# A spectral block on one core: the row transform of x from two fp16 parts in 64-row tiles, and a moved channel mean

## The reference

```python
def conv(x):                                    # x: normalised
    bias = x @ bias_w.T + bias_b
    xf = jnp.fft.rfftn(x.reshape(B, H, W, 4, 96), axes=(1, 2), norm='ortho')
    xr, xi = xf.real, xf.imag
    r1 = relu(block_mul(xr, w1[0]) - block_mul(xi, w1[1]) + b1[0])
    i1 = relu(block_mul(xr, w1[1]) + block_mul(xi, w1[0]) + b1[1])
    r2 = block_mul(r1, w2[0]) - block_mul(i1, w2[1]) + b2[0]
    i2 = block_mul(r2, w2[1]) + block_mul(i1, w2[0]) + b2[1]
    return irfftn(complex(r2, i2), s=(H, W)).reshape(B, H, W, C) + bias
out = x + conv(group_norm(x))                   # 32 groups, eps 1e-5
```

## Time and profile before

| | us |
|---|---|
| median of three runs | 431.16 (430.12 to 432.9) |
| the profiled execution | 432.9 |
| its span, first to last instruction | 431.1 |
| PE busy | 401.2 (93%) |
| DVE busy | 283.1 (66%) |
| ACT busy | 228.9 (53%) |
| POOL busy | 84.1 (19%) |

### The profile page before, as it was taken

One profiled execution on the slowest core, in us unless ns is written; L12 is line 12 of the kernel. 1 busy time (PEld: TensorE's weight loads), 2 busy tenths in 40 slices (PEclk: granted clock), 3 DMA queues, 4 the chain that ended last, 5 costly groups with the idle time before them and its releaser, 6 DMA issues.

```text
span 431.1 us, 19365 instructions
## 1 busy us (share of the span) xinstructions
PE 401.2 (93%) x8610; PEld 354.2 (82%) x8610; DVE 283.1 (66%) x696; ACT 228.9 (53%) x514; POOL 84.1 (19%) x72
## 2 busy tenths in 40 slices
PE   4468799999999999999999999999999999998996
PEld 4467689788898889887898889888898889986894
DVE  4697676864677656874668656865568646767425
ACT  2884865257742666356652576437662666426410
POOL 0000002700063000900036000810027000690000
PEclk9759999999999999999999999999999999999999
DMA  7670000270004300180003600161001700040004
GB/s 220 196 240 2 2 3 5 84 249 2 5 28 171 139 3 3 40 292 4 3 5 122 213 2 5 41 238 57 5 3 68 267 3 5 27 161 2 5 3 148
DMA packets 12406, 33.03 MB, mean 77 GB/s; under 512 B 4962, under 2 KB 6532, under 8 KB 12324
## 3 DMA queue, kind: packets, MB, share of 16 engines
q1 hardware_dynamic: 12324, 31.80, 21.0%
HBM read 16.07 MB, written 12.58 MB: 66 GB/s over the span
## 4 chain that ended last, share of the span: by engine, by line
PE 90%; ACT 4%; issue 2%; DVE 2%; DMA 1%; DVEq 0%; SPq 0%; ACTq 0%
PE bank L571 90%; DMA x_sb<-in_x 1%; ACT y L912 1%; ACT junk L900 1%; ACT yraw L892 1%; ACT r L922 1%; ACT biasw L926 1%; DVE o_sb L1114 0%; ACT w2s L926 0%; DVE r L1098 0%; ACT z L932 0%; ACT junk L903 0%; DVE rho L1029 0%; ACT rho L951 0%; DVE z L1029 0%
## 5 line engine op out<-in xcount | busy, mean ns | idle before, releaser
L571 PE MATMUL bank<-biasw,y 128*64 128x384 f16 x1152 | 111.1, 336 | 0.4 <-issue 0.4
L571 PEld LDWEIGHTS bank<-biasw,y 128*64 128x64 f16 x1152 | 93.4, 196 | 2.5 <-issue 1.0
L571 PE MATMUL bank<-w2s,rho 128*64 128x96 f16 x3072 | 84.9, 207 | 0.0
L571 PEld LDWEIGHTS bank<-w2s,rho 128*64 128x64 f16 x3072 | 80.0, 109 | 4.0 <-issue 2.5
L877 POOL TENSOR_TENSOR x_sb<-x_sb,added 128x384 f32<-128x384 f32 x56 | 74.8, 1370 | 0.0
L571 PE MATMUL bank<-w1R,y 128*128 128x192 f16 (+3 forms) x768 | 60.3, 228 | 5.9 <-ACT y L912 3.2
L1029 DVE SCALAR_TENSOR_TENSOR rho<-bank,rho 128x256 f16<-128x256 f32 (+2 forms) x128 | 39.9, 363 | 34.1 <-ACT rho L951 23.1
L932 ACT ACTIVATE z<-bank 128x384 f16<-128x384 f32 x72 | 35.3, 490 | 49.9 <-PE bank L571 48.9
L875 POOL TENSOR_TENSOR x_sb<-x_sb,added 128x384 f32<-128x384 f32 x8 | 8.1, 1009 | 270.5 <-DVE yraw L1085 270.5
L917 ACT ACTIVATE g<-bank 128x384 f16<-128x384 f32 x64 | 30.0, 480 | 53.4 <-PE bank L571 53.4
L571 PE MATMUL bank<-tab,x_sb 128*128 128x128 f32 x384 | 50.6, 287 | 7.7 <-DMA x_sb<-in_x 6.2
(11 more groups left out here) (109 smaller groups left out, 414.8 us busy)
## 6 DMA issues: line engine op xcount, KB each, us to landing
x_sb<-in_x SPq DMA_DIRECT2D x16, 768.0 KB, 6.7
out<-o_sb SPq DMA_DIRECT2D x14, 768.0 KB, 3.7
y<-y SPq DMA_DIRECT2D x24, 128.0 KB, 2.7
out<-o_sb SPq DMA_DIRECT2D x8, 192.0 KB, 1.9
tab<-in_tab SPq DMA_DIRECT2D x1, 672.0 KB, 5.6
o_sb<-in_bias_wt SPq DMA_DIRECT2D x4, 144.0 KB, 2.9
b1raw<-in_b1h SPq DMA_DIRECT2D x1, 384.0 KB, 5.9
tab<-in_tab SPq DMA_DIRECT2D x1, 292.5 KB, 3.0
```

What stands on the lines that cost most here:

```text
L571: return nc.tensor.matmul(o, lhsT, rhs, start=start, stop=stop, **kw)
```

## The change

Five things are changed together.

1. For images 2 to 7 the row transform `p1` is replaced by `p1_rows`: x is split beforehand into two fp16 parts in a new buffer `x16`, scaled by a power of two near 32 divided by the root of its sum of squares, and each item is made of 24 fp16 matmuls of 64 rows by 64 columns against a new table `widthx`. The items stand behind units 2 to 7 of `c1`, not behind it, and take banks 5 and 6 or 0 and 1. `p3_half(0)` moves from in front of unit 6 to in front of unit 8 and waits for all six copies. Image 0 keeps the old order, and with it `p1` for image 1.
2. The split needs new steps: ACT's `x_square` (two, with a sum), PE's `x_sum` (one small fp32 product), DVE's `x_clamp`, ACT's `x_sqrt`, DVE's `x_scales`, ACT's `x_high` (two), all in the `c2` stage one image earlier, and DVE's `x_low` (two) behind z_low(0) and z_low(2).
3. `channel_means(b + 1)` moves on DVE from behind rho's low parts to between r's and rho's (images 1 to 6).
4. `group_mean` becomes one matmul against a joined table; `shared` prepares its operand in two DVE steps, twice an image.
5. x has three buffers and takes the output in place of `o_sb`; loads are issued one image earlier and wait for the store of the buffer; POOL's `add_map(b)` waits for z_low(0) of its own image.

The diff, cut to its core:

```diff
@@ spectral_block_kernel
-        x_sb = [sb(f"x_sb{p}", [128, TILES, CH]) for p in range(2)]
+        x_sb = [sb(f"x_sb{p}", [128, TILES, CH]) for p in range(3)]
+        x16 = sb("x16", [128, 2, TILES, CH], f16)
-        o_sb = sb("o_sb", [128, TILES, CH])
-        def rho_bank(j, more):
+        def rho_bank(j, more, first):
             if j < 6:
-                at = (2, 0 if more else 4)[j % 2]
+                at = ((0, 2) if more and not first else (2, 0) if more else (2, 4))[j % 2]
+        def p1_pair(m):
+            at = (5, 0)[m % 2]
+            return psum[:, at:at + 2, :].rearrange("k b (x c) -> k (b x) c", x=2)[:, :, 0:128]
@@ sync
-            load(1, 1)
+            load(1)
...
             block3_rows(0, 0)
+            sp.wait_ge(w2_forms, 12)
+            sp.wait_ge(bias_ready, 1 + NT)
+            load(2)
             for b in range(BATCHES - 2):
                 block3_rows(b + 1, (b + 1) % 2)
                 store(b)
-                load(b + 2, b % 2)
+                if b + 3 < BATCHES:
+                    load(b + 3)
@@ tensor
+            def p1_rows(b, m):
+                h, ct = m // NT, m % NT
+                if m == 0:
+                    pe.wait_ge(gl_ready, 8 * b)
+                if m == 1:
+                    pe.wait_ge(o_ready, 8 * b)
+                    pe.wait_ge(dve_step, NSTEP * (b - 1) + VAR_READ)
+                if m >= 2:
+                    pe.wait_ge(y_raw, Y_ITEMS * b + m - 1)
+                if ct == 0:
+                    pe.wait_ge(xl_ready, 2 * (b - 2) + h + 1)
+                bank = p1_pair(m)
+                for i in range(4):
+                    t = 4 * h + i
+                    for of, w in ((0, 0), (0, 1), (1, 0)):
+                        for j in range(2):
+                            rows = slice(64 * j, 64 * j + 64)
+                            last = mm(bank[:, 2 * j:2 * j + 2, 32 * i:32 * i + 32], x16[rows, of, t, 128 * ct:128 * ct + 128],
+                                      widthx[rows, w, 0 if t == 0 else 1, :], of == 0 and w == 0, of == 1, skip_group_check=True)
+                last.then_inc(y_prod, 1)
             def group_mean(src, at):
-                mm(y_bank[0][:, at:at + NT], own, src[:, 0:NT], True, False)
-                return mm(y_bank[0][:, at:at + NT], block3, src[:, NT:NT + 1].to_broadcast([128, NT]), False, True)
+                return mm(y_bank[0][:, at:at + NT], groups, src[:, :], True, True)
@@ c1
-                    if u == 6:
-                        p3_half(b, 0, first)
+                    if u == (8 if more and not first else 6):
+                        p3_half(b, 0, more, first)
...
                     last.then_inc(z_prod, 1)
+                    if more and not first and 2 <= u < 8:
+                        p1_rows(b + 1, u - 2)
@@ p3_half
+                    if more and not first:
+                        pe.wait_ge(y_raw, Y_ITEMS * (b + 2))
@@ p4
+                    if more and not first:
+                        if j == 1:
+                            pe.wait_ge(rl_ready, 9 * b + 6)
+                        elif 2 <= j < 6:
+                            pe.wait_ge(rhoh_ready, 8 * b + j - 1)
+                            pe.wait_ge(rhol_ready, 8 * b + j - 1)
+                        elif j == 7:
+                            pe.wait_ge(rhoh_ready, 8 * b + 6)
+                            pe.wait_ge(rhol_ready, 8 * b + 6)
@@ tensor, image
                 for m in range(Y_ITEMS):
-                    if more:
+                    if first:
                         p1(b + 1, 1 - p, m)
...
+                    if gi == 5 and b + 2 < BATCHES:
+                        x_sum(b + 2)
@@ gpsimd
-                pool.wait_ge(dve_step, NSTEP * min(b + 2, BATCHES))
+                pool.wait_ge(rl_ready, 9) if b == 0 else pool.wait_ge(zl_ready, 9 * b + 1)
                 add_map(b)
@@ scalar, image
+                    if more and not first and 2 <= u < 8:
+                        y_copy_rows(b + 1, u - 2)
-                    for v in {5: (0, 1), 6: (2,), 7: (3,)}.get(u, ()):
+                    for v in ({7: (0, 1), 8: (2, 3)} if more and not first else {5: (0, 1), 6: (2,), 7: (3,)}).get(u, ()):
                         r_high(b, v)
...
                 g_high(b, 2, more)
+                if split:
+                    x_square(b + 2, 0)
                 if more:
                     std(b + 1)
                 g_high(b, 3, more)
+                if split:
+                    x_square(b + 2, 1)
                 for gi in range(4, 7):
                     if more:
                         y_high(b + 1, 1 - p, gi - 4)
+                    if split and gi == 6:
+                        x_sqrt(b + 2)
                     g_high(b, gi, more)
+                if split:
+                    x_high(b + 2, 0)
+                    x_high(b + 2, 1)
                 g_high(b, 7, more)
@@ vector
+            def shared(b, k, src, out):
+                stat(b, k)
+                step(nc.vector.tensor_scalar(src[:, NT:NT + 1], src[:, NT:NT + 1], fourth[:, 0:1], None, ALU.mult))
+                stat(b, k + 1)
+                step(nc.vector.scalar_tensor_tensor(out=out[:, :], in0=src[:, 0:NT], scalar=fourth[:, 1:2],
+                                                    in1=src[:, NT:NT + 1].to_broadcast([128, NT]), op0=ALU.mult, op1=ALU.add))
+            def x_low(b, h):
+                dve.wait_ge(xh_ready, 2 * (b - 2) + h + 1)
+                flat = "k t c -> k (t c)"
+                low(x16[:, 1, 4 * h:4 * h + 4, :].rearrange(flat), x_sb[b % 3][:, 4 * h:4 * h + 4, :].rearrange(flat), xscale[:, :],
+                    x16[:, 0, 4 * h:4 * h + 4, :].rearrange(flat)).then_inc(xl_ready, 1)
@@ vector, image
+                    if more and not first and u in (0, 2):
+                        x_low(b + 1, u // 2)
...
+                if more and not first:
+                    channel_means(b + 1)
                 for j in range(8):
                     dve.wait_ge(rho_prod, 8 * b + j + 1)
...
-                if more:
+                if first:
                     channel_means(b + 1)
                 g_low(b, 0, more)
...
                 for gi in range(4, 7):
+                    if split and gi == 6:
+                        x_clamp(b + 2)
                     if more:
                         y_low(b + 1, 1 - p, gi - 4)
+                    if split and gi == 6:
+                        x_scales(b + 2)
                     g_low(b, gi, more)
```

More of the change, by code:

```diff
@@ L185, in constants @@
     put("width", width.reshape(2, 128, 128).transpose(1, 0, 2))
+    lines = width.reshape(2, 2, 64, 2, 16, 2, 2)
+    assert not lines[:, 0, :, :, :, 1].any() and not lines[:, 1, :, :, :, 0].any()
+    lines = np.stack([lines[:, j, :, :, :, j] for j in range(2)])
+    put("widthx", H_SCALE * lines.transpose(0, 2, 1, 5, 3, 4).reshape(128, 128))
     put("height", P_SCALE * hgt.transpose(1, 0, 2))
@@ L192, in constants @@
     put("inv_low", G_EVAC * inv.astype(np.float16))
-    put("own", own)
-    put("block3", block3)
+    fourth = np.arange(128)[:, None] % 4 == 3
+    put("groups", own + block3)
+    put("fourth", np.concatenate([fourth, ~fourth], axis=1))
     put("const", np.broadcast_to(const, (128, 64)))
@@ L330, in g_bank @@
             return y_bank[gi] if gi < 2 and not more else c_bank[gi % 3]
-        x_loaded = [[sem(f"x_loaded{p}{h}") for h in range(2)] for p in range(2)]
+        x_loaded = [[sem(f"x_loaded{p}{h}") for h in range(2)] for p in range(3)]
+        x_sq = sem("x_sq")
+        x_total = sem("x_total")
+        x_summed = sem("x_summed")
+        x_root = sem("x_root")
+        x_scaled = sem("x_scaled")
+        xh_ready, xl_ready = sem("xh_ready"), sem("xl_ready")
+        ones_ready = sem("ones_ready")
         width_in = sem("width_in")
@@ L398, in spectral_block_kernel @@
         xf, xi = T("xf"), T("xi")
+        widthx = T("widthx").rearrange("k s (a m) -> k s a m", a=2)
         inv, inv_low = (T(name).rearrange("k s (a m) -> k s a m", a=2) for name in ("inv", "inv_low"))
-        own = T("own")
-        block3 = T("block3")
+        groups = T("groups")
+        fourth = T("fourth")
         const = T("const")
@@ L609, in mm3, with c1 @@
                 return mm(o, S[1], W[0], False, stop, **kw)
-            def c1(b, p, first):
+            def c1(b, p, more, first):
                 pe.wait_ge(yh_ready, NT * b + 2)
@@ L661, in shift_product, with p3_half @@
                 last.then_inc(shift_prod, 1)
-            def p3_half(b, half, first):
+            def p3_half(b, half, more, first):
                 if half == 0:
@@ L734, in p4 @@
                         pe.wait_ge(rl_ready, 9 * b + (4, 8, 9)[j // 3])
-                    bank = rho_bank(j, more)
+                    bank = rho_bank(j, more, first)
                     if j < 6:
@@ L808, in image @@
             def image(b, p, more=True, first=False):
-                c1(b, p, first)
+                c1(b, p, more, first)
                 for m in range(Y_ITEMS):
```

(23 more changed lines are left out.)

103 lines of the change are left out of this document (69 added, 34 removed).

## The result

| | us |
|---|---|
| kernel before, median of 4 runs | 431.5 |
| changed kernel, median of 4 runs | 463.73 (463.11 to 465.35) |
| ratio to before | 1.0748 (95%: 1.0717 to 1.078) |
| forecast | 455 (442 to 470) |
| profiled execution and its span | 463.11, 461.3 |

The direction, the place and the size of the waits came as forecast; 463.7 lies in the range, 8.7 above the number. What was missing in the number is a second loss that stood among the rivals: PE's clock falls behind the longest wait, in each of the six images of the profiled execution.

What follows compares the result with a forecast made beforehand. PE, busy 93% of the span, was taken as the bound. 3.92 + 0.28 - 0.27 = 3.93 us an image, +23.6 over six, took the profiled 432.9 to 456.5; with the median 1.7 below, 455 us (442 to 470).

Steps and rivals of the forecast that it cites:

- The matmuls: Row transform on PE: 0.54 us an item (bounds 0.40 and 0.68), 3.24 for 5.81 an image, a gain of 2.57.
- The chain: PE waits for copies from `c1` to `p4`: j = 2 comes 3.92 us later, j = 3 another 0.28, an image.
- What moves at nothing: ACT, DVE, SP and POOL: added steps and earlier loads cost nothing; `x_high` 3.7 us just fits, x_low(0) stays 1.83.
- signs of being wrong: `p4` without idle before j = 2, granted clock of 0.5 in images 1 to 6, or `x_low` rows away from 1.8 us.
- The clock: Rival, chance 0.13: PE's clock falls in the idle time ahead of `p4`'s j = 2, giving 463 to 466 us.
- the sum: Whole kernel: 3.92 + 0.28 - 0.27 = 3.93 us more an image, images 1 to 6, +23.6 in all.
- The rival's price: Half clock behind j = 2's wait: 1.4 us or more lost an image, 8 to 11 in all; chance 0.13.
- a slow x_low(0): Upper bound on DVE: x_low(0) slowed beside POOL to 2.74 us, 0.91 more an image.
- items at 0.68: Upper bound on PE: price of the form change paid twice an item, 0.84 us more an image.
- a late g_high(7): Upper bound on ACT: `x_high` without cover makes g_high(7) and `p6` late, up to 0.5 us.
- The image taken as the measure: The PE, DVE and ACT timelines of one undisturbed image, image 4, were followed; its 3.93 us applied to images 1 to 6.

Runs made afterwards that it cites:

- the channel means' run: Kernel before with only channel_means(b + 1) moved between r's and rho's low parts: 446.77 us, ratio 1.0345.
- the filler: Changed kernel plus 12 matmuls of 128 x 384 without use in front of the wait of p4's j = 2: 455.99 us.

## Why the prediction was right, and where it was short

**The matmuls.** Right. 24 matmuls and the unit behind them come every 1.55 us (255.39 to 256.94); with 1.01 for the unit an item is 0.54, the value taken. A unit follows 0.45 us after an item's start (254.29 behind 253.84), and the other 0.1 us lie between the unit and the next item: a price is there, but within the 0.54 and not the 0.68. The Trainium skill, "TensorEngine Tiling (Array Packing)", section "Key Properties", puts a drain at each change of form; the 0.1 us agree.

**The chain.** Right in each step. Idle time ahead of the first item was forecast at 1.3 and is 1.09; before `p3_half(0)` 0.8 and 0.85; before `p3_half(1)` 0.9 and 1.03; before j = 1 0.4 and 0.36; before j = 2 "nearly 3" and 2.90. j = 2 was put at 23.84 after the start of `c1` and comes at 23.95. For j = 3 0.28 was added, and j = 2 and 3 take 0.24 longer. Undoing the means' place, and changing x_low's, gave back what the waits of 2.90 and 1.09 us cost, so these two are shown as causes and not only seen beside the loss. The other three (0.85, 1.03 and 0.36) are read from the trace; no run removes one of them alone, and they go together where the old order, with its banks and waits, is back.

**What moves at nothing.** Right for ACT: `x_high` takes 3.04 us for two, less than the 3.7 estimated, and g_high(7) waits for PE as before. Right for x_low(0): 1.81 us, unslowed, as it is issued first. x_low(1) took 2.58 beside POOL's additions, one of the prediction's signs of being wrong, but with nobody waiting for it.

**The clock.** This is the step that was short. I kept it apart as a rival with 0.13, because windows of before showed idle time of 1.5 of 4 us at full clock, and took the sum at full clock throughout. The wait of 2.90 us is followed by the half clock in all six images of the profiled execution; a granted clock of 0.5 was among the prediction's signs of being wrong. The row held against it did not settle the matter: in the channel means' run above the clock fell behind 1.54 us in some images and not in others. The rival's price (1.4 us or more an image, 8 to 11 in all, 463 to 466) was right: the filler gives back about 1.5 an image where it keeps the clock up, 6 x 1.5 = 9.0 us. That the forecast's own range reaches 463.7 is luck: its upper end stood for a slow x_low(0), items at 0.68 and a late g_high(7), and none of these came.

The filler run and the six falls show that idle time between bursts brings the half clock back. The Trainium skill, "TensorE: Matmul & The Clock Gate", section "Why this matters for your kernels", warns of such idle gaps, and agrees in that; but here the clock fell behind shorter waits than those that it names, 1.54 to 2.90 us, and the measurement decides.

**The image taken as the measure.** The forecast and this rival were not alternatives: 6 x 3.93 + 9.0 = 32.6 on the profiled 432.9 makes 465.5, and 463.1 was profiled. The sum took image 4 of the kernel before, 48.99 us, for all six. By the starts of `c1`, its images 1, 3 and 5 took 49.97, 50.80 and 49.66, which makes the six 3.5 us longer than six times image 4. Each of these three has a stall of PE in its last unit of `c1`, of 0.68, 1.52 and 0.46 us, for which the profile names no releaser:

```profile
195.04 0.45 PE L571 MATMUL bank<-w1R,y 128*32 128x96 f16 x20 [1.52 <-issue]
```

None of the changed kernel's six images has one. What ends these stalls, and why they are not there in the changed kernel, no run shows. The other way round, about 0.1 us an image and 0.4 outside the six images are missing in the sum.

## What to carry to other kernels

Work that is taken out of a stretch may be the cover of a copy chain: before moving it, add up the chain that it hid (PSUM to ACT to DVE and back, several times), and not only the matmul time that it frees. On an engine that works in the order of its code, what stands in front of a step for which PE waits can cost its full length, even if the engine has idle time elsewhere: here the means took 2.99 us and PE waited 2.90, and 1.54 for 2.56 where the cover was still there. And where a forecast has a new wait of some us on PE, count the clock with it: here it cost about 1.5 us an image on top of the 2.90. And take more than one image as the measure of the kernel before.

## What the runs showed of the hardware that was not expected

A wait of 1.54 us on PE was followed by the half clock in two of six images and left it full in four. One of 2.90 us was followed by it in six of six images in the changed kernel, but in four of five with x_low(0) first, where image 3 kept it full. One of 1.63 us in image 7 was followed by it with x_low(0) first, and not in the changed kernel. So the length of the wait alone doesn't decide, and what else does stays open. Work without use put into the wait kept the clock up there and made the kernel 7.7 us faster.

POOL's first tile, which starts while x_low(0) is on DVE, took 2.51 us, and 1.00 in image 7, where there is no x_low:

```profile
252.04 2.51 POOL L953 TENSOR_TENSOR x_sb<-x_sb,added 128x384 f32<-128x384 f32 x1 [43.88 <-DVE z L1144]
...
415.50 1.00 POOL L953 TENSOR_TENSOR x_sb<-x_sb,added 128x384 f32<-128x384 f32 x1 [43.39 <-DVE z L1144]
```

The 1.5 us more are about the rest of x_low(0), which ends at 253.69, 1.65 us after the tile's start. The rule of the Trainium skill ("SBUF — State Buffer", "SBUF: two separate sides") that the one that comes second waits for the whole instruction agrees.
